# Six transformer layers as one written-out stream of tiles, with the feed-forward between the attention tiles

## The reference

```python
for i in range(DEPTH):                      # DEPTH = 6
    x = attn_layer(shift_tokens(x), Wqkv[i], q_scale[i], k_scale[i], Wo[i]) + x
    x = ffn_layer(shift_tokens(x), ln_g[i], ln_b[i], W1[i], b1[i], W2[i], b2[i]) + x

def attn_layer(x, Wqkv, qs, ksc, Wo):       # 16 heads of 64
    q, k, v = split heads of x @ Wqkv
    q, k = l2norm(q) * qs, l2norm(k) * ksc
    q, k = rotary(q) * scale, rotary(k) / scale
    out = local_attention(q, k, v)          # own and previous window of 32, masked softmax
    return out @ Wo

def ffn_layer(x, g, bln, W1, b1, W2, b2):   # 128 -> 2 x 341 -> 128
    a, gate = split((layernorm(x) * g + bln) @ W1 + b1)
    return a * jax.nn.gelu(gate, approximate=False) @ W2 + b2
```

## Time and profile before

| | us |
|---|---|
| median of 3 runs | 4459.96 (4459.77 to 4462.57) |
| the profiled execution | 4460.07 |
| its span in the trace | 4458.3 |
| PE busy (share of the span) | 3846.2 (86%) |
| DVE busy | 3501.2 (79%) |
| ACT busy | 3407.2 (76%) |
| POOL busy | 2377.6 (53%) |

### The profile page before, as it was taken

One profiled execution on the slowest core, in us unless ns is written; L12 is line 12 of the kernel. 1 busy time (PEld: TensorE's weight loads), 2 busy tenths in 40 slices (PEclk: granted clock), 3 DMA queues, 4 the chain that ended last, 5 costly groups with the idle time before them and its releaser, 6 DMA issues.

```text
span 4458.3 us, 132631 instructions
## 1 busy us (share of the span) xinstructions
PE 3846.2 (86%) x49248; PEld 2440.5 (55%) x49248; DVE 3501.2 (79%) x7236; ACT 3407.2 (76%) x9277; POOL 2377.6 (53%) x1420
## 2 busy tenths in 40 slices
PE   5999999869997699977899877999679997789977
PEld 2444444446664366653566634666436665366653
DVE  6999999679994689954899747999369995589964
ACT  3999999759995489963899836999349995389973
POOL 2444444357772377741777605777137773277750
PEclk8999999989998899988999989999889998899998
DMA  1000000013332033330333302333113332033330
GB/s 45 8 8 10 8 8 26 1 43 81 85 84 55 23 78 83 84 80 7 72 84 82 81 23 56 84 85 81 43 34 81 85 84 65 13 77 84 83 71 19
DMA packets 146282, 245.44 MB, mean 55 GB/s; under 512 B 43664, under 2 KB 69264, under 8 KB 144912
## 3 DMA queue, kind: packets, MB, share of 16 engines
q1 hardware_dynamic: 146064, 242.61, 22.9%
HBM read 26.43 MB, written 2.10 MB: 6 GB/s over the span
## 4 chain that ended last, share of the span: by engine, by line
PE 42%; ACT 27%; SPq 10%; issue 8%; DVE 7%; DMA 3%; POOL 2%; DVEq 0%; ACTq 0%; POOLq 0%
ACT arena L856 12%; PE ps L607 7%; PE ps L722 6%; ACT arena L872 5%; PE ps L556 5%; PE ps L551 5%; ACT arena L831 4%; PE ps L676 4%; PE ps L497 4%; SPq L336 3%; PE ps L731 3%; SPq L346 3%; PE ps L492 3%; DMA arena<-arena 3%; ACT arena L843 2%
## 5 line engine op out<-in xcount | busy, mean ns | idle before, releaser
L607 PE MATMUL ps<-WB,arena 128*128 128x512 f32 x2304 | 1102.3, 615 | 95.0 <-ACT arena L872 37.8
L856 ACT ACTIVATE arena<-arena,nmx 128x64 f32<-128x64 f32 x3072 | 1022.7, 337 | 12.1 <-DVE arena L1145 11.7
L607 PEld LDWEIGHTS ps<-WB,arena 128*128 128x128 f32 x2304 | 418.9, 195 | 510.8 <-issue 451.8
L431 POOL TENSOR_TENSOR arena<-arena 128x1024 f32<-128x1024 f32 x192 | 455.4, 2372 | 400.1 <-DVE arena L1075 397.9
L440 POOL TENSOR_TENSOR arena<-arena,rr 128x1024 f32<-128x1024 f32 x192 | 367.6, 1915 | 466.7 <-DVE rr L1139 466.7
L1068 DVE TENSOR_TENSOR arena<-ps,tables 128x1024 f32<-128x1024 f32 x384 | 468.5, 1220 | 168.9 <-ACT arena L831 168.5
L856 ACT ACTIVATION_READ_ACCUMULATOR arena<-arena,nmx 128x1 f32 x3072 | 585.6, 191 | 0.0
L676 PE MATMUL ps<-arena 128*64 128x64 f32 x12288 | 431.5, 232 | 132.8 <-DMA arena<-arena 108.4
L831 ACT ACTIVATE arena<-ps 128x1024 f32<-128x1024 f32 x384 | 388.5, 1015 | 177.1 <-PE ps L607 142.4
L676 PEld LDWEIGHTS ps<-arena 128*64 128x64 f32 x12288 | 408.6, 146 | 159.6 <-issue 157.4
L1075 DVE TENSOR_TENSOR arena<-ps,tables 128x512 f32<-128x512 f32 x768 | 491.1, 681 | 0.0
(11 more groups left out here) (101 smaller groups left out, 6751.8 us busy)
## 6 DMA issues: line engine op xcount, KB each, us to landing
arena<-arena SPq DMA_DIRECT2D x768, 128.0 KB, 2.3
arena<-arena SPq DMA_DIRECT2D x1536, 64.0 KB
WB<-wb SPq DMA_DIRECT2D x6, 2176.0 KB, 8.6
arena<-X SPq DMA_DIRECT2D x384, 32.0 KB, 1.8
arena<-wa SPq DMA_DIRECT2D x8, 581.0 KB, 3.7
WF<-wf SPq DMA_DIRECT2D x6, 537.5 KB, 3.8
keep<-xT SPq DMA_DIRECT2D x1, 2048.0 KB, 7.7
outT<-keep SPq DMA_DIRECT2D x1, 2048.0 KB, 6.3
```

The lines of the kernel that those rows point to most:

```text
L431: pool.tensor_tensor(tu[:, K], t1[:, K], t2[:, K], ALU.add).then_inc(addk_r, 1)
L607: i = pe.matmul(banks[:, c, :], xs_[r], WB[:, w * INNER + c * COL:w * INNER + (c + 1) * COL], start=True, stop=True)
L856: i = act.activation(pe3[:, :, h, :], sc[:, 64 * h:64 * h + 64].rearrange("p (k q) -> p k q", k=2), ACT.Exp, bias=nmx[:, h:h + 1], accum_o ...
```

## The change

The six layers become one stream of 192 tiles (`TILES`), all of it written out in Python: each step s of 206 stands in the program with its own constants, the hardware loops over layers, steps and batches of this half are gone, and with them the register work for counts and addresses. The first tile of a layer follows the last tile of the layer before.

The feed-forward is cut into 48 chunks of four tiles (512 tokens). Chunk q is worked at in steps 4q + 6 to 4q + 11, between the parts of the attention tiles: step +6 brings its input (two transfers on SP), +7 turns it and takes statistics and unit, +8 turns it back and normalises it, +9 makes gate and value three times, +10 the down product and the residual. It uses only banks 2 and 3, in the part of a step in which q has been rotated; the next step's query projection waits for the feed-forward's last use. Weights are reloaded in parts (k and scales, q, v, Wo, WF), each when the last tile of a layer has used it. The output is stored in eight parts. ACT squares k and q one behind the other, ahead of the exponents; before, the first four exponents stood between them.

```diff
-HEAD, TAIL = range(-2, 3), range(NT - 2, NT + 3)
+TILES = LAYERS * NT
+PER = COL // P
+FF = TILES // PER
+LAG = 12
...
+        FF_BANK = 2, 3
+
+        fx, fn, gate, *hf = rings[2 * RING:]
...
+        def chunk(s, lag):
+
+            return (s - lag) // PER if (s - lag) % PER == 0 and 0 <= s - lag < TILES else None
...
+            def keys_in(l):
+                need(sp, k_mm, NT * l)
+                weights(l, INNER, 2 * INNER, lk)
+                need(sp, tab_r, 4 * l)
+                weights(l, B_SC, B_W, ls)
...
+            def xs(t):
+                c = tile_col(t)
+                need(sp, v_mm, t - RING + 1)
+                need(sp, xs_r, 32 * t)
+                need(sp, fin_r, t // PER - NT // PER + 1)
...
+            def ff_in(q):
+                c = tile_col(PER * q)
+                sp.wait_ge(y_r, PER * q + PER)
+                need(sp, fb_mm, q)
+                need(sp, fx_in, 32 * q)
...
+            for s in range(-2, TILES + LAG):
+                l = (s + 2) // NT
+                new = 0 < l < LAYERS
+                if live(s + 2):
+                    xs(s + 2)
+                if live(s - 2):
+                    widen(s - 2)
+                if new and (s + 2) % NT == 0:
+                    keys_in(l)
+                    queries_in(l)
...
+                if chunk(s, 6) is not None:
+                    ff_in(chunk(s, 6))
+                if live(s):
+                    vshift(s)
...
+            def queries_of(t):
+                first(t, lq)
+                need(pe, rotq_r, t)
+                for q, lag, count, each in ((chunk(t - 2, 7), 7, fn_r, 1), (chunk(t - 2, 8), 8, xn_r, 1),
+                                            (chunk(t - 2, 9), 9, hf_r, MF), (chunk(t - 2, 10), 10, fin_r, 1)):
+                    if q is not None:
+                        pe.wait_ge(count, each * (q + 1))
+                product(t, 0, q_ps, q_mm)
...
+            def ff_gate(s, q, m):
+                if m == 0:
+                    pe.wait_ge(xn_r, q + 1)
+                    q_free(s)
+                else:
+                    pe.wait_ge(gate_r, MF * q + m)
+                pe.matmul(ps[0:FW[m], FF_BANK[0], :], WF[:, HID + m * P:HID + m * P + FW[m]], fn,
+                          start=True, stop=True).then_inc(g_mm, 1)
...
+                if live(s):
+                    turn_q(s)
+                    values_of(s)
+                if chunk(s, 10) is not None:
+                    ff_down(s, chunk(s, 10))
+                if chunk(s, 7) is not None:
+                    ff_turn(s, chunk(s, 7))
+                if chunk(s, 9) is not None:
+                    ff_gate(s, chunk(s, 9), 0)
+                if live(s):
+                    scores(s)
+                if chunk(s, 9) is not None:
+                    ff_value(chunk(s, 9), 0)
+                if live(s - 2):
+                    attend(s - 2)
...
+                if chunk(s, 8) is not None:
+                    ff_back(s, chunk(s, 8))
...
+                if live(s):
+                    turned_q(s)
+                if live(s - 1):
+                    exponents(s - 1, range(8, 12))
+                    exponents(s - 1, range(12, 16))
+                if chunk(s, 9) is not None:
+                    ff_gelu(chunk(s, 9), 0)
+                if live(s):
+                    values(s, 0)
+                if chunk(s, 9) is not None:
+                    ff_gelu(chunk(s, 9), 1)
+                if live(s):
+                    values(s, 1)
+                if chunk(s, 9) is not None:
+                    ff_gelu(chunk(s, 9), 2)
...
+                if live(s + 1):
+                    norms(s + 1)
+                if chunk(s, 10) is not None:
+                    ff_final(chunk(s, 10))
+                if chunk(s, 9) is not None:
+                    ff_hidden(chunk(s, 9), 0)
+                if live(s - 1):
+                    inverse(s - 1)
+                if live(s):
+                    masked(s)
+                if chunk(s, 7) is not None:
+                    ff_unit(chunk(s, 7))
+                if chunk(s, 9) is not None:
+                    ff_hidden(chunk(s, 9), 1)
+                    ff_hidden(chunk(s, 9), 2)
```

More of the change, by code:

```diff
@@ L195, in hold, with live, need @@
             eng.sem_inc(passed, 1)
[L197 to L210 removed]
+        def live(t):
+            return 0 <= t < TILES
+        def chunk(s, lag):
+            return (s - lag) // PER if (s - lag) % PER == 0 and 0 <= s - lag < TILES else None
+        def need(eng, s, v):
+            if v > 0:
+                eng.wait_ge(s, v)
         def on(c):
@@ new lines, in first, with product, keys_of @@
+            def first(t, count):
+                if t % NT == 0:
+                    pe.wait_ge(count, 16 * (t // NT + 1))
+            def product(t, w, banks, count):
+                for c in range(2):
+                    i = pe.matmul(banks[:, c, :], xs_[t % RING], WB[:, w * INNER + c * COL:w * INNER + (c + 1) * COL],
+                                  start=True, stop=True)
+                i.then_inc(count, 1)
+            def keys_of(t):
+                first(t, lk)
+                pe.wait_ge(xs_r, 32 * (t + 1))
+                if t >= 2:
+                    pe.wait_ge(v_r, t - 1)
+                elif t == 1:
+                    pe.wait_ge(rotk_r, 1)
+                product(t, 1, kv_ps, k_mm)
```

805 lines of the change are left out of this document (390 added, 415 removed).

## The result

The changed kernel takes 4072.02 us, the median of 4 runs (4065.07 to 4075.82), beside 4459.86 (4457.67 to 4462.57) for the kernel before: a ratio of 0.913, 95% interval 0.911 to 0.914. The direction was forecast; the gain is 388 us where 149 were, and the time lies 8 us under the low end of the range. The profiled execution took 4075.82, its span is 4074.0.

What follows compares the result with a forecast made beforehand. PE, DVE and ACT were all taken as full at 13.34 us a tile, so only vanishing stages pay; 925.7 + 2884 (tiles) + 404 (chunks) + 13.5 + 52 + 26 + 4 + 1.8 = 4311 us, range 4080 to 4450.

Steps and rivals of the forecast that it cites:

- Point 1: ACT's squares in each tile: ACT idles until q is projected, +0.7 us per tile, making 14.05.
- Point 2: PE's instruction fetch: written-out code stops PE in three of four tiles, raising the tile from 14.05 to 15.1 us.
- the first rival: PE's instruction fetch: code arrives in time, no stops, 13.85 us a tile, 4115 us in all; chance 0.28.
- Point 3: Feed-forward inside the attention tiles: 8.6 us per chunk of four tiles, summed tile by tile.
- e: Feed-forward in the stream: the surcharge per chunk of four tiles, forecast 8.6 us, counted 47 times.
- Point 4: Layer seams: weights reloaded in parts cost 0, at most 5 us per layer; tables on DVE 2.7 us, five times, 13.5.
- Point 5: Kernel's end: one drain of 52 us, last chunk 26, last add and store 4, outside the span 1.8.
- A: Rival on the tile stream: no stops, 13.85 us a tile, 9.5 a chunk, chunk period 65, 4115 us; chance 0.28.
- p: Attention stream: the period of one tile without chunk surcharge, forecast 15.1 us, counted 191 times.
- B: Rival on PE: stops also lower its clock, 16.0 us a tile, chunk period 73, 4502 us; chance 0.11.
- C: Rival on the feed-forward: the gate, GELU, product chain is longer, 13.8 us a chunk, 4555 us; chance 0.06.
- D: Rival on queue order: SP waiting for a chunk's end holds up tiles; no chance of its own given.

Runs made afterwards that it cites:

- e2: The changed kernel without its feed-forward and the waits for it, so the output lacks those updates: 3785.68 us, ratio 0.849.
- e8: The kernel before with only ACT's squares of k and q put one behind the other, ahead of the exponents: 4570.52 us, ratio 1.024.
- e3: The changed kernel with the first four exponents put back between ACT's squares of k and q: 4138.2 us, ratio 0.928.
- e1: The kernel before with only the loop over a layer's middle tiles written out: 4545.81 us, ratio 1.019.
- e7: The changed kernel making only one of the three down products, so the result is incomplete: 4074.27 us, ratio 0.913.
- e5: The changed kernel with GELU replaced by Identity, so no table loads are needed in the stream: 4056.0 us, ratio 0.910.
- e4: The changed kernel with the projection of v moved to between the scores and the product with v: 4281.8 us, ratio 0.960.
- e9: The changed kernel with the third gate and value pair moved to the down tile and the down product to the statistics tile: 4164.3 us, ratio 0.936.

## Why the prediction missed

**What bounds the kernel, and that only vanishing stages pay:** right in the first half. The stages went, and nothing new appeared at the ends.

**Point 1, order on ACT (+0.7):** right. Tiles without a stop take 14.1 in e2 (14.05 forecast), and e8 gives 0.57 in loops. ACT's idle time ahead of the square of q is 0.7 us in the changed kernel (median of 192), as forecast. What the step overlooked is that with the feed-forward it is a gain (e3: 66 us).

**Point 2, written-out code (+1.05):** right in mechanism, mis-sized. e1 shows the loss by itself, 0.78 in a steady tile. Stops came in 53% of the tiles of e2, not three in four, and cost 1.0 where 1.4 were taken: 14.1 + 0.53 x 1.0 = 14.6, not 15.1. I had read the rate off three tiles, two of which stopped. The whole trace of before has 36 stops, but these are six places of the ten written-out steps, the same six in each layer; they depend on where the blocks end in the code, and the changed kernel meets all positions in turn. This is 0.48 x 191 = 92 us of the miss. The page "Runtime: NRT & Kernel Launch" of the Trainium skill, section "Instruction fetch mechanics", on which the first rival rested, is not borne out: the runs of straight-line code have the stops. The two experiments by themselves add up to 13.34 + 0.57 + 0.78 = 14.69, where e2, which has both, has 14.62.

**Point 3, the walk through a chunk (8.6):** the step that failed. A chunk costs 6.0, 47 x 2.6 = 122 us of the miss. The walk added each engine's work to the path of a tile that points 1 and 2 had already made longer. In fact much of it fell into the waits that those had opened: against 14.62, the turn-back tile is 1.7 us shorter, the down tile 0.1 shorter, the gate tile 5.6 and the statistics tile 2.4 longer. By its terms: gate 5.6 (4.3), down -0.1 (1.8), statistics 2.4 (2.0), turn-back -1.7 (0.5). The gate tile was priced too low, and by another engine: the walk took ACT's load, two GELUs and a last pair, but the chain there is PE's alone, with 5.85 us of products. Statistics was sized about right. The errors that made e too high are the down tile, where PE's 2.7 us and the table load lie beside DVE's work (e7: no change; e5: both loads of a chunk are worth 0.3), and the turn-back tile, which runs at DVE's own pace of 12.7, below even the 13.34 of before, so that ACT's order and the stops cost it little; why it does so, and the tiles of e2 don't, was not tried. The drain of about 1.38 us that the Trainium skill, "ScalarE: Activation LUTs", section "What ACT_TABLE_LOAD costs", adds to a switch does not show: 0.9 us idle ahead of 47 loads, and 16 us in all from leaving 93 out. The two misses of 92 and 122 us, with the 13.5 us for the tables, which the measured 14.62 and 6.0 already contain, are the 227 us of the stream.

**Point 4, tables and parts (13.5, and 0 to 5 a layer):** the chunk with a seam in it (from its down tile on) takes 67.5 us, the others 64.3, 16 us for five seams. The four table products of a seam took more than twice the 2.7 us forecast, here at the first:

```profile
1414.53 5.66 DVE L1135 TENSOR_TENSOR tables<-rotary,WB 128x512 f32<-128x512 f32 x4
```

In each of the five seams the first product took 2.15 us and the second 2.38, the other two 0.68 as before. POOL was working all through the first and for the first 1.84 us of the second, and not during the others, nor during any of the 24 products before (0.68 to 0.69). The mean of the line, 1342 ns, hides this.

**Point 5, ends:** right within 4 us.

**Rivals.** A's time (4115) was nearest, and its sign of a chunk period of 65 came true, but by two errors against each other: stops are there (93 of them), p is 14.62 and not 13.85, and e is not 9.5. B fell: the granted clock over the stream is 0.98, though it was 0.50 for 99 us of it in 26 pieces. C fell; D's waits on SP or DMA do not show (18.7 us in all ahead of the product with v, against 108.4 before).

**What would show it:** 1.9 instruction blocks a tile, as forecast (364 in the 191 periods of the stream); a chunk 64.7 and not 69; stops in half of the tiles and not in three of four; 94 table loads (96 forecast). Those signs named the right terms, which made the size of each readable.

What stays open: what the stops cost in the changed kernel itself. e4 removed three quarters of them only together with a later v, and nothing tried removes them alone. An estimate from the changed kernel's tiles with and without a stop (turn-back 13.0 and 12.8, down 14.9 and 14.0, statistics 17.3 and 16.6, gate 21.9 in four tiles and 20.0) is some 50 us in all; it is a comparison of tiles and not an experiment.

## What to carry to other kernels

Work that is put into a full pipeline costs about its own time on the engine whose chain sets that tile (5.85 us of gate and value products on PE, and a tile 5.6 us longer), and little where it lies beside another engine's work (down products and table loads, near nothing); adding the busy times of the engines, or walking each tile by itself, overstated it here. The same work can change sides: a table load that was nearly free stood on the chain when a GELU was moved (e9). When leaving work out on one engine gives nothing, look for a second chain of the same length before calling the engine free: 0.8 us of DVE a tile was worth 6 us or less alone, and 50 with ACT shortened. Read a rate off as many tiles as the trace has, not off three, and look at the single durations behind a mean.

## What the runs showed of the hardware

PE's stops stand at a fixed place in its code. If weight loads, matmuls and semaphore instructions of PE are counted through the changed kernel, all 93 stops in the bursts stand at the same remainder of a count of 256, to within one instruction, and the 16 KB transfers of the instruction queue fit such blocks (364 transfers and 364 boundaries in the stream, 1.91 a tile). The transfers also show what a stop waits for: in all 93, PE goes on 1.2 to 1.6 us after a transfer of that queue has landed (median 1.4), and so it does in the 36 stops of before, the 91 of e1 and the 105 of e2.

Whether PE stops at a boundary goes with how fast the block before it was used up: of 32 boundaries that came 1 to 2 us after the one before, all stopped (1.9 us on average), of 47 at 2 to 3 us 42 (1.4 us), of 51 at 3 to 6 us 18, and of 148 with 6 us or more one (all 278 boundaries that fall in the two bursts). For the first of these groups the time since the boundary before and the stop add up to 3.6 us on average. The Trainium skill, "Runtime: NRT & Kernel Launch", section "Instruction fetch mechanics", has the block-wise fetch ahead, which agrees, but has it mostly hidden, which the two bursts, 192 weight loads and as many matmuls in some 3.5 us, do not bear out. With products of 512 columns between the bursts (e4) the stops fall to 21.

A 32-bit product on DVE of two operands of 128x512 that both lie in SBUF (the on-chip memory) took 0.68 us with POOL idle and 2.15 to 2.38 us with POOL at work (ten of 24 in the changed kernel).
